# A selective scan and eight experts in one stream: expert tiles of 128 rows, the convolution on VectorE, the last stage by half chunks

## The reference

```python
y = layernorm(xn) * ln_gamma + ln_beta          # second norm
left, right = split(y @ W_up + b_up)            # 2 x 128 channels
left = silu(causal_conv(left, conv_w, 3 taps) + conv_b)
delta = softplus(left @ W_delta + b_delta); B = left @ W_B; C = left @ W_C
# for each of 128 channels and 64 states, over all 4096 rows:
h = exp(delta * A) * h + (delta * left) * B;  s6 = sum_n(h * C) + left * D
s = xn + (s6 * silu(right)) @ W_down + b_down

top2, idx = top_k(xn @ gate, 2); w = softmax(top2)      # 8 experts
g = silu(sum_k w_k * (silu(xn @ w1[e_k]) * (xn @ w3[e_k])) @ w2[e_k])   # inner width 1024
out = x + s * g
```

## Time and profile before

| | |
|---|---|
| median of 3 runs | 1404.51 us (1402.75 to 1405.11) |
| the profiled execution's own time | 1398.48 us |
| its span (first to last instruction) | 1396.4 us |
| PE busy | 1242.4 us, 89% |
| VectorE (DVE) busy | 1191.0 us, 85% |
| GpSimd (POOL) busy | 1114.0 us, 80% |
| ScalarE (ACT) busy | 754.3 us, 54% |
| data moved by DMA | 218.04 MB, mean 156 GB/s |

### The profile page before, as it was taken

One profiled execution on the slowest core, in us unless ns is written; L12 is line 12 of the kernel. 1 busy time (PEld: TensorE's weight loads), 2 busy tenths in 40 slices (PEclk: granted clock), 3 DMA queues, 4 the chain that ended last, 5 costly groups with the idle time before them and its releaser, 6 DMA issues. The chain is left out here.

```text
span 1396.4 us, 21735 instructions
## 1 busy us (share of the span) xinstructions
PE 1242.4 (89%) x5800; PEld 913.5 (65%) x5800; DVE 1191.0 (85%) x1618; ACT 754.3 (54%) x1613; POOL 1114.0 (80%) x1090
## 2 busy tenths in 40 slices
PE   5847799999999999999999999999999999977730
PEld 5725367777777777777777777777677677754410
DVE  6747579998899889988999889988898899988858
ACT  1351566555655575557555675557555755555521
POOL 0356279898999798888998898989997888898863
PEclk9978999999999999999999999999999999975555
DMA  6111265447555646564574457446545564654346
GB/s 209 61 38 46 68 212 175 143 129 220 147 150 150 188 149 181 161 195 130 170 224 136 122 183 222 133 122 220 171 137 168 172 172 138 198 186 130 115 147 229
DMA packets 124965, 218.04 MB, mean 156 GB/s; under 512 B 15264, under 2 KB 40992, under 8 KB 124832
## 3 DMA queue, kind: packets, MB, share of 16 engines
q10 hardware_dynamic: 73728, 134.25, 32.7%
q1 hardware_dynamic: 43616, 61.82, 13.6%
q0 software_dynamic: 7488, 20.46, 4.6%
HBM read 191.57 MB, written 24.90 MB: 155 GB/s over the span
## 5 line engine op out<-in xcount | busy, mean ns | idle before, releaser
L416 POOL TENSOR_TENSOR arena<-arena,c_rep 128x512 f32<-128x512 f32 x512 | 602.4, 1181 | 129.2 <-DVE arena L954 117.0
L954 DVE TENSOR_TENSOR_SCAN arena<-bank,carry,arena 128x512 f32<-128x512 f32 x512 | 652.6, 1275 | 36.9 <-ACT bank L724 34.9
L1189 PE MATMUL bank<-xgT,wring 128*128 128x256 f32 x2240 | 536.5, 382 | 1.0 <-issue 1.0
L1189 PEld LDWEIGHTS bank<-xgT,wring 128*128 128x128 f32 x2240 | 419.0, 190 | 120.3 <-issue 59.9
L724 ACT ACTIVATE bank<-arena,a_neg 128x512 f32<-128x512 f32 x512 | 354.3, 692 | 94.5 <-DVE arena L954 41.0
L945 DVE TENSOR_TENSOR arena<-bank,b_rep 128x512 f32<-128x512 f32 x512 | 351.7, 687 | 47.7 <-PE bank L1202 31.0
L1202 PE MATMUL bank<-stack,pick 128*128 128x512 f32 x512 | 298.3, 589 | 4.7 <-DVE arena L945 4.5
L648 ACT ACTIVATE th<-bank 128x256 f32<-128x256 f32 x312 | 119.2, 382 | 297.1 <-PE bank L1189 222.8
L1158 PE MATMUL bank<-wring,hid 128*128 128x256 f32 x1120 | 270.6, 384 | 2.3 <-POOL hid L431 2.3
L1158 PEld LDWEIGHTS bank<-wring,hid 128*128 128x128 f32 x1120 | 210.4, 191 | 62.7 <-issue 25.2
L431 POOL TENSOR_TENSOR hid<-gt,ue 128x256 f32<-128x256 f32 x312 | 226.9, 727 | 2.0 <-DVE gt L966 1.9
(11 more groups left out here) (167 smaller groups left out, 847.6 us busy)
## 6 DMA issues: line engine op xcount, KB each, us to landing
arena<-delta_d ACTq DMA_DIRECT2D x512, 256.0 KB
wring<-in_w_all SPq DMA_DIRECT2D x64, 384.0 KB, 5.1
arena<-results SPq DMA_DIRECT2D x16, 512.0 KB, 6.3
xn<-in_x SPq DMA_DIRECT2D x4, 1024.0 KB, 9.5
xn_d<-xn SPq DMA_DIRECT2D x4, 1024.0 KB, 5.3
parts_d<-spare SPq DMA_DIRECT2D x16, 256.0 KB
stack<-parts_d SPq DMA_DIRECT2D x16, 256.0 KB
out<-arena SPq DMA_DIRECT2D x8, 512.0 KB, 3.1
```

Of the source, the lines that this page charges most:

```text
L416: pool.tensor_tensor(p_ring[:, s % P_RING, :], h_ring[:, s % H_RING, :], of_chunk(c_rep, c, 2), ALU.mult).then_inc(s_hc, 1)
L954: v.tensor_tensor_scan(out=h_ring[:, s % H_RING, :], data0=a_bank[s % 2][:, :], data1=b_ring[:, s % B_RING, :], initial=carry[:, q:q + 1], ...
L1189: ins = pe.matmul(bank[:, m * SLOT:(m + 1) * SLOT], wring[:, kk, (2 * m + h) * P:(2 * m + h + 1) * P], xgT[:, i % 2, h, :], start=(h == 0) ...
```

## The change

`SLOT` becomes 128. There are now 71 tiles, of which 67 hold rows with these inputs. A step takes two slices of the inner width for 128 rows: eight products of 128 columns in place of four of 256, still one bank, one tanh, one copy, one gate and one product of 256 columns. A tile has 4 steps and takes 7 pairs (empty: 5), with the pairs of its steps and down products in `STEP_PAIR` and `OUT_PAIR`; a down turn is two products of 256 columns. `xg` and `o_sb` alternate between tiles. One indirect DMA gathers a tile, one scatters it.

The convolution of chunks 1 to 7 leaves TensorE (three products, L1074, and the eviction L581) and becomes three operations of VectorE at three pairs. That of chunk 0 stays.

In the last stage seven sets of results are in SBUF: three of them in `wring`, loaded as soon as the last tile is scattered. Tanh writes PSUM banks, and VectorE's three operations go by halves of 512 columns with one operand in PSUM.

```diff
-SLOT = 256
+SLOT = P
+STEPS = KS // 2
+SW = 2 * SLOT
-SETS = 4
+EARLY_SETS, SETS = 3, 7
-LONG_TILES = 35
-LONG, SHORT = 13, 10
+LONG_TILES = 67
+LONG, SHORT = 7, 5
+STEP_PAIR, OUT_PAIR, ROWS_PAIR = ((0, 2, 4, 5), (0, 1, 2, 3)), ((3, 6, 8, 8), (4, 4, 6, 6)), (6, 2)
...
-                for s in range(SH):
-                    n = SH * i + s
-                    pool.indirect_dma_start(xg[:, s, :], None, xn_d,
-                                            bass.IndirectOffsetOnAxis(source[:, n:n + 1], 0)).then_inc(s_xg, 16)
+                pool.indirect_dma_start(xg[:, i % 2, :], None, xn_d,
+                                        bass.IndirectOffsetOnAxis(source[:, i:i + 1], 0)).then_inc(s_xg, 16)
...
+            def conv(c, tap):
+                cv = stage("cv")
+                if tap == 0:
+                    v.wait_ge(s_partd, STORES * c)
+                    v.wait_ge(s_lrev, c + 1)
+                    v.tensor_scalar(cv, of_chunk(c_rep, c, 2), half[:, 2:3], half[:, 3:4], ALU.mult, ALU.add).then_inc(s_taps, 1)
+                else:
+                    v.wait_ge(s_taps, 2 * (c - 1) + tap)
+                    v.scalar_tensor_tensor(out=cv, in0=of_chunk(c_rep, c, 2 - tap), scalar=half[:, 2 - tap:3 - tap],
+                                           in1=cv, op0=ALU.mult, op1=ALU.add).then_inc(s_taps if tap == 1 else s_cvs, 1)
...
+                if s == RESULTS_AT:
+                    sp.wait_ge(s_o, STEPS * TILES)
+                    sp.wait_ge(s_res, 16 * TILES)
+                    for c in range(EARLY_SETS):
+                        load_results(c)
...
+            def mix(c):
+                chain = [last_bank(c, h)[:, :].rearrange("p (n c) -> p n c", c=D) for h in range(2)]
+                v.wait_ge(s_add, 2 * c + 2)
+                ge(v, s_st[c % 4], 16 * (c // 4))
+                for h in range(2):
+                    v.wait_ge(s_tf, 2 * c + h + 1)
+                    v.scalar_tensor_tensor(out=chain[h], in0=chain[h], scalar=1.0, in1=half_rows(result_rows(c, 0), h),
+                                           op0=ALU.add, op1=ALU.mult).then_inc(s_mix, 1)
...
-                pe.wait_ge(s_w[kk], 16 * (i + 1))
+                for k in (2 * j, 2 * j + 1):
+                    pe.wait_ge(s_w[k], 16 * (i + 1))
                 def products():
-                    for m in range(2):
-                        for h in range(2):
-                            ins = pe.matmul(bank[:, m * SLOT:(m + 1) * SLOT], wring[:, kk, (2 * m + h) * P:(2 * m + h + 1) * P],
-                                            xgT[:, i % 2, h, :], start=(h == 0), stop=(h == 1))
+                    for r in range(2):
+                        for m in range(2):
+                            for h in range(2):
+                                ins = pe.matmul(bank[:, m * SW + r * SLOT:m * SW + (r + 1) * SLOT],
+                                                wring[:, 2 * j + r, (2 * m + h) * P:(2 * m + h + 1) * P],
+                                                xgT[:, i % 2, h, :], start=(h == 0), stop=(h == 1))
```

More of the change, by code:

```diff
@@ L38 @@
 PLACED_AT = 6
-LONG_TILES = 35
-LONG, SHORT = 13, 10
-WORK_AFTER = dict(tanh=("conv", 1), sigmoid=("conv", 2), silu=("conv", 3), right=("conv", 4), exp=("delta", 2), ln=("delta", 3),
+LONG_TILES = 67
+LONG, SHORT = 7, 5
+STEP_PAIR, OUT_PAIR, ROWS_PAIR = ((0, 2, 4, 5), (0, 1, 2, 3)), ((3, 6, 8, 8), (4, 4, 6, 6)), (6, 2)
+LOAD_OF = dict(step=4, out=2, rows=1, down=2, delta=2, b=2, c=2)
+WORK_AFTER = dict(conv=("pairs", 14), tanh=("pairs", 17), sigmoid=("pairs", 18), silu=("pairs", 19), right=("pairs", 20),
+                  exp=("delta", 2), ln=("delta", 3),
                   less=("delta", 4), sum=("delta", 5), round=("delta", 10), low=("delta", 11), store=("delta", 13),
                   stack=("delta", 17))
-WORK_PARTS = dict(sum=4)
+WORK_PARTS = dict(sum=4, conv=3)
 BIAS_AT = 61
 def turns_by_pair():
-    by_pair, empty = [[] for _ in range(PAIR_COUNT + 1)], set()
+    by_pair = [[] for _ in range(PAIR_COUNT + 1)]
     by_pair[MOE_FIRST - 1].append(("rows", 0, 0))
@@ L54, in turns_by_pair @@
         first = MOE_FIRST + LONG * min(i, LONG_TILES) + SHORT * max(i - LONG_TILES, 0)
-        spare = [first + 12] if i < LONG_TILES else []
-        for k in range(KS):
-            if i < LONG_TILES:
-                step, out = first + 3 * (k // 2) + k % 2, first + 3 * (k // 2) + (5 if k < 6 else 6)
-            else:
-                step, out = first + k, first + 2 * (k // 2) + 3
-            by_pair[step].append(("step", i, k))
-            by_pair[out].append(("out", i, k))
+        form = int(i >= LONG_TILES)
         if i + 1 < TILES:
-            by_pair[first + (8 if i < LONG_TILES else 4)].append(("rows", i + 1, 0))
-        empty.update(spare)
+            by_pair[first + ROWS_PAIR[form]].append(("rows", i + 1, 0))
+        for j in range(STEPS):
+            by_pair[first + STEP_PAIR[form][j]].append(("step", i, j))
+            by_pair[first + OUT_PAIR[form][j]].append(("out", i, j))
     def next_free(s):
-        free = [p for p in range(s, PAIR_COUNT) if all(kind == "out" for kind, i, k in by_pair[p])]
-        return next((p for p in free if p in empty and p < s + 5), free[0])
+        return next(p for p in range(s, PAIR_COUNT) if sum(LOAD_OF[kind] for kind, i, j in by_pair[p]) <= 2)
     for c in range(NC):
@@ L99, in work_by_pair @@
             for r in range(WORK_PARTS.get(name, 1)):
-                work[PAIR_OF[(kind, c, 0)] + after + r].append((name, c, r))
+                first = PAIRS * (c - 1) if kind == "pairs" else PAIR_OF[(kind, c, 0)]
+                work[first + after + r].append((name, c, r))
     return work
@@ L687, in outs @@
                 for turn, i, k in here:
-                    if turn == "out" and k == KS - 1:
+                    if turn == "out" and k == STEPS - 1:
                         evict_out(i)
@@ L873, in _ @@
             link(v.tensor_tensor(sv, sv, shift.unsqueeze(2).broadcast_to([P, E, NT]), ALU.add))
-            for half_tile in range(SH):
-                v.tensor_scalar(halves[:, :].rearrange("p (t h) -> p t h", h=SH)[:, :, half_tile], start[:, :],
-                                float(P * half_tile), None, ALU.add)
+            v.tensor_copy(tiles[:, :], start[:, :])
             for k, hot in enumerate((hot1, hot2)):
@@ L958, in gates @@
             def gates(here):
-                for turn, i, kk in here:
+                for turn, i, j in here:
                     if turn == "step":
-                        k = KS * i + kk
+                        k = STEPS * i + j
                         v.wait_ge(s_th, k + 1)
@@ L1228, in turns @@
                     if kind == "out":
[L1229 removed]
+                        expert_out(STEPS * t + k)
                         continue
```

213 lines of the change are left out of this document (106 added, 107 removed).

## The result

| | before | after |
|---|---|---|
| median of 4 runs, us | 1403.63 (1400.80 to 1405.11) | 1383.94 (1381.21 to 1387.15) |
| ratio, 95% interval | | 0.9865 (0.9842 to 0.9889) |
| span of the profiled execution, us | 1396.4 | 1382.9 |
| first scan to pair 32 | 107.9 | 106.3 |
| pairs 32 to 485 | 1046.4 (2.31 a pair) | 1063.6 (2.348 a pair) |

The change gains 19.7 us by the medians and 18.9 by the ratio, where 43 were forecast: less than half. The time lies in the stated range and at the very edge of the forecast's own (1338 to 1384). The two profiled executions differ by 13.5 us only, since that of before lay 5 under its median and that of after 1.4 over; the stretches in the table, with the 0.7 us by which the first scan starts later, add up to that.

What follows compares the result with a forecast made beforehand. TensorE was taken to set the pace, at 2.25 of 2.31 us a pair. Gains of 21 (pairs), 2 (head) and 20 (last stage) gave 43 off: 1361 us median, own range 1338 to 1384, eight in ten 1316 to 1402.

Steps and rivals of the forecast that it cites:

- TensorE's floor before, 2.25 under a pace of 2.31: Pairs before the change: TensorE sets the pace, its work 2.25 us a pair and waits 0.06.
- The floor of 2.12 and the pace of 2.22: Pairs after the change: TensorE's work 2.12 us a pair, plus 0.10 of waits; bounds 2.15 and 2.31.
- The convolution on VectorE, 13 us: Chunks 1 to 7: three VectorE operations a chunk at 0.62 us each, 1.9 a chunk, 0.03 a pair.
- stated bound of 18: Convolution's two-operand taps beside GpSimd's additions: at most 14 x 1.3 us = 18 us in the run.
- The record of 128 columns, 0.109: Step's products on TensorE: weight load hides, records 0.109 us apart, a step 1.74 us as before; upper end 0.132.
- Rival 3: Step's weight load shows: records 0.132 us apart, 95 us more, 1456, slower; chance 0.09.
- The weights, 18 us: Changes of expert: TensorE waits 2.5 us at each of 7, 18 us in all; bounds 0 and 9 each.
- The pairs after 485, 2.41 each: Last 26 pairs: 2.41 us each, 63 us, with the same density of turns and low clock.
- 21 forecast from pair 32 to the last scan: Pairs 32 to the last scan: 1087 us with weights where it was 1108, a gain of 21.
- The last stage, 20 us: After the last scan: early-loaded results and half operations, 3.9 us a chunk, end 20 us earlier.
- the first (the relief turns into waits): Middle pairs: pace stays 2.31, 41 us more than forecast, 1402, no change; chance 0.12.
- Its sign, TensorE idle for hidden products in most tiles: Tiles' down products: TensorE waiting for GpSimd's hidden products in most tiles would show relief turned into waits; no size given.

Runs made afterwards that it cites:

- experiment 5: Half of TensorE's gate and up products left out, in both kernels: changed kernel 1337.32 us (ratio 0.9547), kernel before 1351.59 us (0.9638).
- experiment 3: The kernel before with only the changed kernel's last stage, tiles unchanged: 1388.51 us, ratio 0.9910.
- experiment 8: The kernel before with the new last stage and its empty tiles on 8 pairs instead of 10: 1377.72 us, ratio 0.9824.
- experiment 2: The changed kernel with the later chunks' convolution back on TensorE: 1390.49 us, ratio 0.9909.

## Why the prediction was wrong

In its own order:

- **TensorE's floor before, 2.25 under a pace of 2.31: the reading that failed.** It took the busiest engine for the one that sets the pace. With half of its gate and up products gone the pace falls only to 2.21 (experiment 5). Before the change two thirds of the pairs already lasted 2.12 us or less, VectorE's own distance, which is more than the 1.95 of TensorE's ordinary pair, and 84 of 453 lasted over 2.5. After it they are two thirds and 90. Cut each of the 453 pairs at 2.12 us: the part below adds up to 942 us before, 939 after and 937 to 942 in all the kernels here, and the part above to 104 before, 125 after and 64 and 79 in experiment 5. Even 240 us of relief for TensorE took 41 and 46 us from the part above and at most 3 from the part below, and an average over all pairs does not show that.
- **The floor of 2.12 and the pace of 2.22: the step that failed.** The pace was 2.348, 58 us more over 453 pairs (40 with the 18 for weights set against it). What the runs put in its place: the weights 12 us, the two taps 9 and the narrow form 10, each measured alone, and 40 where all three are taken away at once. The remaining 18 to 27 no run takes apart; that they are relief that turned into waits is argued from TensorE's idle time, 0.13 a pair in place of 0.04. TensorE's floor itself came out at 2.215 of busy time: 0.0025 x 64 / 7 = 0.02 is the records, 12 us of doubled time at the lower clock 0.03, and the rest is not taken apart.
- **The copy of the transposed rows, put at nothing.** The prediction counts the pairs from a step to its down product and from a slice's release to its need, but not those from a tile's transposition to its first step: five before, one after. TensorE stood about 24 us for ScalarE's copy there, more than for weights, and in the kernel before not at all between 220 and 1250 us. What that costs no run shows, as none moves the transposition; after the wait of 2.67 us VectorE's scan stood 2.37 us for a decay behind the second table load (L733), so not all of it need be on the path.
- **The convolution on VectorE, 13 us:** it took 27, beyond the stated bound of 18 for its two-operand taps (19.2) and far beyond 0.62 each for the one-operand form (8.1 in place of 4.3). What the Trainium skill says (SBUF — State Buffer, Who interferes with whom) covers the two-operand taps, and names `tensor_scalar`, the one-operand form, among those that can contend in a two-port mode; whichever engine issues first has the shared pair for the whole instruction. The trace agrees: 0.73 and 0.52 begun just before GpSimd's product, and otherwise an end 0.3 to 0.6 us after GpSimd's own. That its time would not be hidden was named, and left out of the sum.
- **The record of 128 columns, 0.109:** right, 0.1115. Rival 3 is refuted, and with it, for these float32 products, the 81 against 56 ns of the Trainium skill (TensorE: Matmul & The Clock Gate, Back-to-back issue gap).
- **The weights, 18 us:** right in place and about in size (12; 1.8 before, not clear of zero). TensorE's waits named for a DMA sum to 13.7 in 11 waits.
- **The pairs after 485, 2.41 each:** they took 54.2/26 = 2.09, 8 us better. The density of turns is that of before, as taken (four steps in five pairs). But TensorE waited 14.9 us for GpSimd's hidden products between 1270 and 1333 us in the kernel before, in pairs of up to 4.5 us, and 4.4 us between 1287 and 1342 after; VectorE was 96% busy there.
- **The last stage, 20 us:** 22. First mix and halves within 0.1 us; a chunk took 3.59 where 3.9 were taken.

So the sum: 2 forecast and 1.6 measured at the head, 21 forecast and -9.4 from pair 32 to the last scan, 20 forecast and 22 in the last stage. Of the rivals, the first (the relief turns into waits) is nearest for the middle. Its sign, TensorE idle for hidden products in most tiles, did not show: 12 such waits. The largest waits are for ScalarE's copy and for weights.

The whole by parts, from the ratios of experiments 3, 8 and 2 and of the change: the last stage's halves -12.6 us, shorter empty tiles and early loads -12, tiles of 128 rows with the convolution on TensorE +12 (the size of what the weights cost), the convolution on VectorE -6; in all the -19 of the change. Each is a difference of two ratios and uncertain by 4 to 6 us.

Open: what the wait for the transposed rows costs, and with it what is left of the 58 us. The stretches at 1.2 GHz stand beside TensorE's standstills, of which this wait made three and weights two of the six; without reloads they are 23.9 us too, so the weights alone do not make them.

## What to carry to other kernels

An engine's busy share is not the pace's floor where three engines hand each item on and stand within a tenth of each other: before costing a relief of the busiest, take the second's distance from item to item as the floor and look at how many items already keep it. Add the moved work at its price beside the engine that it waits for, not alone, and count it as not hidden. When a schedule is made tighter, count the distance in items for every hand-over, also for the small copies of an engine that is half idle. A buffer that is read by two stages can be loaded in the parts that each stage frees.

## What the runs showed of the hardware

- A 512-column operation on VectorE with one SBUF operand took 0.52 us when it began 0.16 us before GpSimd's product, 1.16 on average and up to 2.57 when GpSimd was there first. With the first operand in a bank the last stage's halves took 0.68 to 0.70 each, 0.60 from start to start, with GpSimd's sum beside them and without.
- VectorE writing its result into a bank costs nothing more: two halves in 1.29 us (L1039), and 1.28 into SBUF (L1044).
- A wait marked issue can be one for a semaphore that the profile does not attribute: all 30 of TensorE's before a step ended 0.09 us after ScalarE's copy.
- The granted clock fell to 1.2 GHz between 150 and 1200 us for 23.9 us in all in the changed kernel, for none in the kernel before, and for 74 us with half the gate and up products left out of the kernel before (85 in the changed one).
